# A running sum moved from matmuls to a VectorE scan, and a new start with unsplit weights, in a gated slot attention block

## What is computed

```python
q, k = rope(hs @ Wq.T), rope(hs @ Wk.T)          # per head, 128 wide
v, g = hs @ Wv.T, hs @ Wg.T
s = clip(hs @ Ws1.T @ Ws2.T + bs2, -32, 32)      # (B, H, T, 64)
es = exp(s); enz = exp(-cumlogsumexp(s, axis=T)) # enz = 1 / running sum of es over T
A = where(mask, q @ k.T * DK ** -0.5, 0)
qv = softmax(enz * (A @ es))
W2 = where(mask, (qv * enz) @ es.T, 0)
o = rmsnorm(W2 @ v) * g_norm_weight * silu(g)
x = layernorm(hs + o @ Wo.T)
out = layernorm(x + x @ (weight * scale[:, None]).T + bias)
```

## Time and profile before

| | |
|---|---|
| median of three runs | 1446.03 us |
| profiled execution | 1446.81 us, span 1445.0 us |
| TensorE busy | 1413.9 us, 98% |
| VectorE busy | 948.9 us, 66% |
| ScalarE busy | 510.4 us, 35% |
| GpSimd busy | 513.9 us, 36% |
| mean granted TensorE clock | 0.994 |

### The profile page before, as it was taken

One profiled execution on the slowest core, in us unless ns is written; L12 is line 12 of the kernel. 1 busy time (PEld: TensorE's weight loads), 2 busy tenths in 40 slices (PEclk: granted clock), 3 DMA queues, 4 the chain that ended last, 5 costly groups with the idle time before them and its releaser, 6 DMA issues.

```text
span 1445.0 us, 23200 instructions
## 1 busy us (share of the span) xinstructions
PE 1413.9 (98%) x9320; PEld 1176.2 (81%) x9320; DVE 948.9 (66%) x1629; ACT 510.4 (35%) x1048; POOL 513.9 (36%) x440
## 2 busy tenths in 40 slices
PE   5999999999999999999999999999999999999998
PEld 4888888888888888888888888888888888888776
DVE  5756666676766657567765656667665666657677
ACT  4333233234332323333332333324433332323446
POOL 3322333334343333234533323433532343332245
PEclk9999999999999999999999999999999999999999
DMA  5211112122211202112220211122121111201223
GB/s 196 85 44 37 60 44 74 31 95 103 66 59 45 73 23 74 44 66 88 102 74 23 74 45 37 59 74 103 52 102 45 37 59 44 74 23 67 66 102 117
DMA packets 39561, 97.04 MB, mean 67 GB/s; under 512 B 4384, under 2 KB 4512, under 8 KB 35616
## 3 DMA queue, kind: packets, MB, share of 16 engines
q1 hardware_dynamic: 36864, 90.85, 18.8%
q10 hardware_dynamic: 2592, 4.72, 0.9%
HBM read 74.58 MB, written 20.97 MB: 66 GB/s over the span
## 4 chain that ended last, share of the span: by engine, by line
PE 93%; DVE 3%; POOL 1%; ACT 1%; issue 1%; DMA 0%; SPq 0%; POOLq 0%; ACTq 0%; DVEq 0%
PE bank_kg L969 24%; PE bank_qv L969 14%; PE bank_a L969 12%; PE bank_t L1001 5%; PE bank_a L1031 4%; PE bank_wo L1231 4%; PE bank_qv L989 4%; PE bank_qv L986 4%; PE bank_qv L988 4%; PE bank_c L1238 3%; PE bank_e L1014 3%; PE bank_wo L1207 3%; PE bank_wo L1142 2%; PE bank_wo L1211 1%; PE bank_wo L1146 1%
## 5 line engine op out<-in xcount | busy, mean ns | idle before, releaser
L479 POOL TENSOR_TENSOR rms<-var,minus_half 128x4 f32<-128x4 f32 x64 | 65.2, 1018 | 537.9 <-DVE var L938 537.9
L969 PE MATMUL bank_kg<-w_hi,hs_hi 128*128 128x512 f32 x512 | 207.6, 406 | 1.9 <-DVE w_lo L702 1.9
L969 PE MATMUL bank_kg<-w_hi,hs_lo 128*128 128x512 f32 x512 | 202.6, 396 | 0.0
L969 PE MATMUL bank_kg<-w_lo,hs_hi 128*128 128x512 f32 x512 | 201.9, 394 | 0.0
L969 PE MATMUL bank_a<-wo_hi,oT 128*128 128x512 f32 x512 | 174.8, 402 | 0.0
L986 PE MATMUL bank_qv<-hs_hi,w_hi 128*128 128x256 f32 x504 | 146.4, 290 | 9.1 <-DVE w_lo L702 9.1
L784 DVE RECIPROCAL enzT<-cumsT 128x256 f32<-128x256 f32 x64 | 112.2, 1753 | 63.8 <-ACT cumsT L571 51.8
L447 POOL TENSOR_TENSOR kv<-rope_a,rope_b 128x512 f32<-128x512 f32 x64 | 82.7, 1293 | 177.7 <-DVE rope_b L732 177.7
L989 PE MATMUL bank_qv<-hs_hi,w_lo 128*128 128x256 f32 x504 | 141.0, 280 | 0.0
L988 PE MATMUL bank_qv<-hs_lo,w_hi 128*128 128x256 f32 x504 | 140.9, 280 | 0.0
L442 POOL TENSOR_TENSOR qT<-rope_a,rope_b 128x512 f32<-128x512 f32 x64 | 82.7, 1292 | 159.7 <-DVE rope_b L744 159.7
(11 more groups left out here) (179 smaller groups left out, 3258.5 us busy)
## 6 DMA issues: line engine op xcount, KB each, us to landing
w_raw<-w_groups SPq DMA_DIRECT2D x28, 1024.0 KB, 5.0
hs_raw<-hs_cols SPq DMA_DIRECT2D x64, 256.0 KB, 2.8
x_scratch<-part SPq DMA_DIRECT2D x64, 256.0 KB, 2.0
part<-x_scratch SPq DMA_DIRECT2D x48, 256.0 KB, 2.7
part<-hs_rows SPq DMA_DIRECT2D x16, 256.0 KB, 3.7
w_raw<-x_scratch SPq DMA_DIRECT2D x16, 256.0 KB, 3.5
w_raw<-w_groups SPq DMA_DIRECT2D x14, 256.0 KB, 6.2
out<-gate ACTq DMA_DIRECT2D x8, 256.0 KB, 2.1
```

The lines of the kernel that those rows point to most:

```text
L479: pool.tensor_tensor(rms[:, :], var[:, :], minus_half[:, :], ALU.pow).then_inc(rms_made, 1)
L969: mm = pe.matmul(dst, x, y, start=start and n == 0, stop=stop and n == 2, **kw)
```

## The change

The running sum: TensorE only transposes es (`turn_es`, two transposes in fp32 instead of four products), ScalarE copies the result to `esT`, and VectorE makes `cumsT` from it with two `tensor_tensor_scan` instructions (multiply by one, add), which start from 0 or the last column of the chunk before, ahead of the reciprocal. The split of es on ScalarE and GpSimd, the two copies to `cumsT` and [identity | keep] go; a memset of ones comes.

The start: the products of chunk 1 (and Q of chunk 2) take raw weights and rows in fp32, one product for three, and wait for the loads (`first_in`) alone. The quarters of all four weights have buffers of their own (`first_raw`: Wv in kv[1] and qT[1], Wg in o_sq, o_gated, states and gate[1]), so that SP issues all loads in a row. The splits are still made, for later chunks: those of Wv among VectorE's work of the start, those of Wg in step 1, with waits on TensorE in step 1 for each. Chunk 1 itself is no longer split. Chunk 4 is rounded behind kT, and the bulk of ws2's rest is made at the end of step 1.

The last step: VectorE splits x1T 0 ahead of okT and x1T 2 behind mask_w2, and the other work of tick 2 stands behind ok_shifted on VectorE and behind the exp of prob on ScalarE. TensorE does ffn 2 ahead of the transposes of the last o_gated.

```diff
@@ -333,30 +339,31 @@
             def load_first(m, k):
-                cols, _, _ = first_quarter(m, k)
-                sp.dma_start(w_raw[SLOT[m]][:, cols], w_groups[0, m][:, cols]).then_inc(first_in[SLOT[m]][k], 16)
-            load_hs(0, 0)
+                sp.dma_start(first_raw[m][k], w_groups[0, m][:, first_cols(k)]).then_inc(first_in[m][k], 16)
+            sp.dma_start(hs_first[:, :], hs_cols[0]).then_inc(first_hs_in, 16)
+            load_first(WQ, 0)
             load_hs(1, 1)
-            for k in (0, 2):
-                load_first(WQ, k)
+            load_first(WQ, 2)
             for k in range(KT):
...
             for k in range(KT):
-                sp.wait_ge(first_lo_made, KT * WQ + k + 1)
                 load_first(WV, k)
...
             for k in range(KT):
-                sp.wait_ge(first_lo_made, KT * WK + k + 1)
                 load_first(WG, k)
-            for slot in range(2):
-                sp.wait_ge(hs_lo_made, slot + 1)
-                sp.wait_ge(u_mm, slot + 1)
-                load_hs(slot, slot + 2)
-            sp.wait_ge(first_lo_made, KT * WG + KT)
+            load_hs(0, 2)
+            sp.wait_ge(q_mm, 2)
+            sp.wait_ge(u_mm, 2)
+            sp.wait_ge(hs_lo_made, 2)
+            load_hs(1, 3)
+            sp.wait_ge(k_mm, 1)
+            sp.wait_ge(first_lo_made, KT * WK + KT)
             load_w(WO, 0)
+            sp.wait_ge(g_mm, 1)
...
@@ -533,72 +533,51 @@
                 for k in range(KT):
-                    cols, loaded, _ = first_quarter(m, k)
-                    act.wait_ge(first_in[SLOT[m]][k], loaded)
-                    copy(w_hi[m][:, cols], w_raw[SLOT[m]][:, cols]).then_inc(first_hi_made, 1)
+                    act.wait_ge(first_in[m][k], 16)
+                    copy(w_hi[m][:, first_cols(k)], first_raw[m][k]).then_inc(first_hi_made, 1)
...
                 act.activation(es[slot][:, :], s_clip[:, :], ACT.Exp).then_inc(es_made, 1)
-                act.wait_ge(es_made, n)
-                copy(es_hi[slot][:, :], es[slot][:, :]).then_inc(es_hi_made, 1)
...
-            def two(ap):
-                return ap.rearrange("p (r t) -> p r t", r=2)
-            def turned(slot, n, first):
-                act.wait_ge(sumT_mm, n)
-                copy(two(esT[:, :]), esT_acc).then_inc(esT_made, 1)
-                if first:
-                    copy(two(cumsT[slot][:, :]), cumsT_acc).then_inc(cumsT_made, 2)
-                else:
-                    for r in range(2):
-                        act.activation(cumsT[slot][:, P * r:P * r + P], cumsT_acc[:, r, :], ACT.Identity,
-                                       bias=cumsT[1 - slot][:, P * r + P - 1:P * r + P]).then_inc(cumsT_made, 1)
 ...
-            hs_split(1)
-            hs_split(2)
+            hs_split(2, 2)
             first_hi(WQ)
...
             act.wait_ge(const_in, 16)
-            u_hi(1)
-            u_hi(2)
             first_hi(WV)
-            copy(ident_keep[:, 0:P], ident).then_inc(consts_made, 1)
-            copy(ident_keep[:, P:2 * P], keep).then_inc(consts_made, 1)
             act.wait_ge(ws2_in, 16)
             ws2_hi(0, H)
+            u_hi(1)
+            act.wait_ge(ws1_in, 16)
+            copy(ws1_of(0), ws1_tiles()).then_inc(ws1_hi_made, 1)
             first_hi(WG)
+            u_hi(2)
+            hs_split(3)
             exp_s(0, 1)
-            copy(ws1_of(0), ws1_tiles()).then_inc(ws1_hi_made, 1)
-            hs_split(3)
-            hs_split(4)
             from_bank(kv_of(0, 1), per_head(bank_qv[:, :]), v_mm, 1, v_made)
...
             act.activation(gate[0][:, :], bank_kg[:, :], ACT.Tanh, scale=0.5).then_inc(th_made, 1)
-            turned(0, 1, True)
+            from_bank(esT[:, :], esT_acc, esT_mm, 1, esT_made)
             from_bank(kT[:, :], bank_t[:, :], kT_mm, 1, kT_made)
+            hs_split(4)
             ws2_hi(H, GROUPS * H)
...
@@ -779,7 +760,16 @@
-            def make_enz(slot, n):
+            def make_enz(slot, n, first):
+                dve.wait_ge(esT_made, n)
+                if first and n == 1:
+                    dve.wait_ge(ones_set, 1)
+                for r in range(2):
+                    initial = 0.0 if first else cumsT[1 - slot][:, P * r + P - 1:P * r + P]
+                    cols = slice(P * r, P * r + P)
+                    dve.tensor_tensor_scan(cumsT[slot][:, cols], ones[:, :], esT[:, cols], initial, ALU.mult, ALU.add
+                                           ).then_inc(cumsT_made, 1)
                 dve.wait_ge(cumsT_made, 2 * n)
@@ -798,21 +788,21 @@
             rotate_q(1, bank_qv)
+            first_lo(WV, 0, 1)
             dve.wait_ge(q_summed, 1)
...
             u_lo(1)
+            first_lo(WV, 1, 2)
+            rotate_k(0, 1)
+            ws2_lo(0, H, 2)
             u_lo(2)
-            first_lo(WV)
-            ws2_lo(0, H, 2)
-            rotate_k(0, 1)
             clip(1)
-            first_lo(WG)
-            make_enz(0, 1)
+            first_lo(WV, 2, 4)
+            dve.wait_ge(ws1_hi_made, 1)
+            minus_hi(ws1_of(1), ws1_tiles(), ws1_of(0)).then_inc(ws1_lo_made, 1)
+            make_enz(0, 1, True)
             make_gate(0, 1)
             mask_a(1)
-            dve.wait_ge(ws1_hi_made, 1)
-            minus_hi(ws1_of(1), ws1_tiles(), ws1_of(0)).then_inc(ws1_lo_made, 1)
-            ws2_lo(H, GROUPS * H, 5)
...
@@ -877,14 +870,17 @@
+                if not left:
+                    x1T_split(0, 0)
                 dve.wait_ge(okT_mm, i)
...
                     lo(oT_lo, bank_t[:, :], oT_hi, oT_hi_made, i - 1, oT_lo_made)
-                if not left:
-                    tick(2, 2)
                 if has_low_rank(i):
                     u_lo(i + 3, 2)
+                if i == 1:
+                    first_lo(WG, 0, 2)
                 if last and c == 3:
@@ -892,6 +888,8 @@
                                   ).then_inc(ok_shifted, 1)
+                if not left:
+                    tick(2, 2, split=False)
                 if left:
@@ -903,6 +901,8 @@
                                          ).then_inc(eps_scaled, 1)
+                if i == 1:
+                    first_lo(WG, 2, 4)
                 if last and c == 1:
@@ -923,8 +923,10 @@
                 mask_w2(i)
+                if not left:
+                    x1T_split(2, 2)
                 if left:
-                    make_enz((c + 1) % 2, n)
+                    make_enz((c + 1) % 2, n, c == CB - 1)
                     make_gate((c + 1) % 2, n)
@@ -939,6 +941,8 @@
                     mask_a(n)
+                if i == 1:
+                    ws2_lo(H, GROUPS * H, 5)
                 if c == 0:
...
@@ -1005,15 +1009,11 @@
-            def turn_and_sum(slot, n):
-                pe.wait_ge(es_hi_made, n)
-                pe.wait_ge(es_lo_made, n)
+            def turn_es(slot, n):
+                pe.wait_ge(es_made, n)
                 for r in range(2):
-                    for x, half in enumerate((es_hi, es_lo)):
-                        mm = pe.matmul(bank_e[:, 2 * P * r:2 * P * r + 2 * P], half[slot][:, P * r:P * r + P],
-                                       ident_keep[:, :], start=x == 0, stop=x == 1)
-                mm.then_inc(sumT_mm, 1)
+                    mm = pe.transpose(esT_acc[:, P * r:P * r + P], es[slot][:, P * r:P * r + P], ident)
+                mm.then_inc(esT_mm, 1)
@@ -1045,44 +1045,49 @@
...
                 for k in range(KT):
-                    pe.wait_ge(first_lo_made, KT * m + k + 1)
-                    mm = product(dst[:, :], chunk_tile(1, k), cols((w_hi[m], w_lo[m]), F * k, F),
-                                 start=k == 0, stop=k == KT - 1)
+                    pe.wait_ge(first_in[m][k], 16)
+                    mm = pe.matmul(dst[:, :], hs_first[:, P * k:P * k + P], first_raw[m][k], start=k == 0,
+                                   stop=k == KT - 1)
                 return mm
-            pe.wait_ge(hs_hi_made, 2)
-            pe.wait_ge(hs_lo_made, 2)
+            pe.wait_ge(first_hs_in, 16)
             for k in range(KT):
-                pe.wait_ge(first_lo_made, KT * WQ + k + 1)
-                for n, dst in ((1, bank_qv), (2, bank_a)):
-                    mm = project_q(n, dst, k)
-                    if k == KT - 1:
-                        mm.then_inc(q_mm, 1)
+                pe.wait_ge(first_in[WQ][k], 16)
+                for e, hs in enumerate((hs_first, hs_raw[1])):
+                    if k == 0 and e == 1:
+                        pe.wait_ge(hs_in[1], hs_loaded(2))
+                    for n, dst in ((1, bank_qv), (2, bank_a)):
+                        for x in range(2):
+                            head = slice(P * (2 * (n - 1) + x), P * (2 * (n - 1) + x) + P)
+                            at = P * (2 * x + e)
+                            mm = pe.matmul(dst[:, at:at + P], first_raw[WQ][k][:, head], hs[:, P * k:P * k + P],
+                                           start=k == 0 and at == 0, stop=k == KT - 1, skip_group_check=True)
```

(23 more changed lines are left out.)

93 lines of the change are left out of this document (48 added, 45 removed).

## The result

The kernel after takes 1420.26 us (median of four runs, 1419.81 to 1420.74), the kernel before 1446.01 beside it: a ratio of 0.982, with a 95% interval of 0.981 to 0.984. That is 25.8 us less, where 31.4 were predicted; 1414.6 was the forecast, and the range ended at 1420.0.

A forecast was written before the change was run, and what follows sets the result against it. TensorE, busy 98% of the span, was taken to bound the kernel. Loop 22.0, start 4.3 and last step 5.1 sum to 31.4 us, so 1446.0 becomes 1414.6 us; range 1409 to 1420.

The forecast's parts named there:

- The loop: Running sum in each step: two transposes replace four products on TensorE, 0.35 us per call, 63 calls, 22.0 us.
- Rival 5: Between mask_w2 and o_gated VectorE becomes the bound, deciding from 1.9 us per scan; 1472 at 2.1 us each; chance 0.03.
- The start: Everything up to step 1 and its waits: step 1 5.2 us sooner, less 0.9, a gain of 4.3 us.
- (a): Start: TensorE's first product, after the first hidden chunk and first quarter of Wq, at 6.2 us instead of 9.09.
- (b): Start: Q as 32 fp32 products of 0.247 us, 2.7 us of it at half speed, ending at 15.4.
- (c): Start: K takes 3.9 us and ends at 19.3; V follows the low-rank product, without the 3.76 us hole.
- (d): Start: VectorE's chain of rotations, u and splits is late; G starts at 25.3, against 35.23 before.
- (e): After G: TensorE waits 1.1 us for hs_lo(4); step 1 starts at 32.8 instead of 38.05, 5.2 us sooner.
- (f): Step 1: Wg's splits on VectorE make TensorE wait about 0.9 us for G.
- The first rival: The start gives nothing: VectorE's chain and late chunk 4 eat it, or the clock falls; 1418.9 us, chance 0.10.
- The last step: Step 64: ffn 0 follows the ok transposes without the wait and at the high clock, 5.1 us.
- The second rival: The tail gives only its wait, since the low clock came before the hole; 1417.3 us, chance 0.07.

The follow-up runs named there:

- the old start: The kernel after with the start of before put back (split products for the first chunk, first loads behind their splits): 1424.07 us.
- the old last step: The kernel after with the last step's order of before put back: 1424.71 us.
- three working edits: The kernel after with twelve products of ones during the first loads, chunk 4 rounded ahead of the gate, and scans reading their bank: 1418.99 us.

## Why the prediction was right or wrong, step by step

**The loop, 22.0: mis-sized, 17.7.** The failed step is "the trace has exactly this elsewhere": the 0.22 us for two transposes and the change of kind, taken from L1250 and carried to another place. At L1250 it is right, and the 0.57 for the four products is right too. But L1250 stands behind 128-row products, and the transposes of es stand behind W2 and o, which are 64-row products. There the first transpose takes 0.17 us to the next start, not 0.11, the median of all calls in both traces. So pair and change cost 0.28, not 0.22, and a call saves 0.57 - 0.28 = 0.29, not 0.35. Over 63 calls the 0.06 makes 3.7 of the 4.3 us that are missing. The rest is 0.01 us a step (intervals 0.281 shorter, where the place itself gives 0.29), spread over other rows, and stays unexplained. The experiments bear it out: the pair ahead of W2 starts without the 0.06 and G pays for the place instead, and a second pair costs 0.22. Whether it is the 64 rows or something else that these products have in common isn't tested.

The split of the 0.22 was wrong as well, at no cost to the sum. The second transpose of L1250 by itself, with the product behind it (kernel before):

```profile
611.17 0.27 PE L1250 MATMUL bank_e<-small_ops,states 128*128 128x128 f32 x1
611.20 0.36 PE L986 MATMUL bank_qv<-hs_hi,w_hi 128*128 128x256 f32 x1
```

It starts 0.11 behind the first, the product starts 0.03 behind it and takes 0.20 instead of 0.12. So the pair's own price is the whole 0.22, and the 0.08 "for the change of kind" is the end of the second transpose, which shows in the row behind. "0.14 us" is a distance between two starts and not a price, and the expectation of the run with the transposes twice took it for one again. The bound "if fp32 here cost like a plain product of L1031" puts a product for a transpose: a product there is two records of 0.11, a transpose one.

**The changes of weights: not seen, 1.4 lost.** The prediction priced every pair of scans at 0.8, covered. In general that was right: a scan is 0.41 us from zero and 0.47 from a carried value, pairs 0.74 and 0.86, TensorE never waits for masked or o_gated in ordinary steps, and the reciprocal's wait of the earlier trace rows is gone. What I left out was GpSimd beside the scan. I had used "u (1.46 beside GpSimd)" in the start, a VectorE operation on SBUF operands that was four times too long, and didn't ask where in the loop a long GpSimd operation meets the scans. The eps_sum of the kernel before, as long as es_lo in 54 of 64 steps, said the same, and I hadn't read that row. In the kernel before, VectorE had nothing to be held at the place of the scans: mask_w2 reads a bank, and the reciprocal has one operand.

**The shape of that rival.** Rival 5 looked for VectorE as the bound in every step, and only a scan of 1.9 us would do it. It came true in 3 steps of 63, with a scan of 2.5 us, and by GpSimd.

**The start, 4.3: 4.5 in spans, by errors that cancel.** (a) 6.58, not 6.2. (b) The slow pace lasted 4.9 us and not 2.7, which cost 1.1 more; but a product takes 0.223 and not 0.247, which gave 0.8 back: Q ended at 16.1, predicted 15.4. (c) K took 3.5 us, not 3.9, and V followed without a hole. (d) VectorE's chain: G at 26.03, predicted 25.3, and TensorE waited 1.31 for the split of ws2 as that step says. (e) Step 1 at 32.99, predicted 32.8, behind a wait for hs_lo(4) of 0.74 that rounding chunk 4 sooner takes away. (f) Step 1's G waited 0.38 for Wg's split, not 0.9. The first rival (nothing from the start) fell by the old start, and the third (a clean start) didn't happen. (The 2.3 us more for Q in the first rival should be 2.1: 7.9 less 48 x 0.12.)

**The last step, 5.1: 5.2.** Wait and clock both, as the old last step shows. The second rival fell with it: the low clock came in the wait or right behind it, and without the wait it didn't come. The trace of before could have told: the 0.85 over the earlier trace rows is 1.00 until the wait was well under way, and about half behind that (windows as in rows 8):

```profile
1372.00:1373.80 1.80, 0.43 (x4) 0.19 (x2) 1.32 (x3) 0.90 (x2) 0.29 (x1) 1.00 0.00 0
1373.80:1374.60 0.80, 0.00 (x0) 0.03 (x1) 0.77 (x3) 0.00 (x0) 0.00 (x0) 0.52 0.00 0
```

That its length varies from run to run I hadn't seen; the traces of before that I read showed only one length.

**The sign** was right, and 98% of TensorE's time as the bound held. The range missed by 0.3 us because it took in the bounds of start and last step, but no dearer transposes: 0.06 us a call moves the sum by 3.7.

## What to carry to other kernels

A short TensorE operation has a price of its own and a price of its place. Take the first from the longest run of that operation in the trace, divided, and not from one distance between starts at a border between kinds, where its end can stand in the row behind. Take the second from a place with the same neighbour ahead; single records in a narrow window show it. When an operation with two SBUF operands is put on VectorE, look in every kind of step, the rare ones too, for what GpSimd runs beside it; one operand in a bank takes the hold away. And when a wait is put into an in-order queue, list what stands behind it in the start as well as in the loop: here one copy behind one wait ate 3.9 us of three working edits, the low clock behind the wait included.
